# A four-layer graph network on one core: bias and fold products of the recurrent steps in the upper column half

## The reference, cut to what matters

```python
def step(feat, _):
    transformed = jnp.einsum('nd,khd->knh', feat, W) + b[:, None, :]
    msgs = transformed[etypes, src]
    a = jax.ops.segment_sum(msgs, dst, num_segments=num_nodes)
    feat = _gru_cell(a, feat, w_ih, w_hh, b_ih, b_hh)
    return (feat, None)
```

## Time and profile before

| | before |
|---|---|
| median of 3 runs | 13580.82 us |
| lowest and highest | 13574.45, 13581.73 us |
| the profiled execution | 13563.08 us |
| its span | 13561.3 us |
| TensorE, busy share of the span | 81% |
| VectorE, ScalarE, GpSimd | 41%, 26%, 32% |
| DMA queue q1, share of 16 engines | 39.6% |

### The profile page before, as it was taken

One profiled execution on the slowest core, in us unless ns is written; L12 is line 12 of the kernel. 1 busy time (PEld: TensorE's weight loads), 2 busy tenths in 40 slices (PEclk: granted clock), 3 DMA queues, 4 the chain that ended last, 5 costly groups with the idle time before them and its releaser, 6 DMA issues.

```text
span 13561.3 us, 260962 instructions
## 1 busy us (share of the span) xinstructions
PE 10980.6 (81%) x61679; PEld 6352.3 (47%) x61680; DVE 5577.2 (41%) x21369; ACT 3538.1 (26%) x9563; POOL 4391.2 (32%) x3429
## 2 busy tenths in 40 slices
PE   2888888799877777777777777775899999999999
PEld 2444444333335555555555555554644444444443
DVE  6888888766624333433343344343311111111111
ACT  0666666533302222222222222222100000000000
POOL 2000000000007888888888888885000000000000
PEclk7666676699889999999999999998699999999999
DMA  2444444422273333333333333336399899899898
GB/s 99 140 138 137 137 137 137 148 90 104 77 282 38 42 42 42 42 42 42 42 42 42 42 42 42 42 42 37 132 352 347 336 352 348 335 351 348 336 350 306
DMA packets 1120503, 2096.75 MB, mean 155 GB/s; under 512 B 373089, under 2 KB 982914, under 8 KB 1012531
## 3 DMA queue, kind: packets, MB, share of 16 engines
q1 hardware_dynamic: 823768, 1913.47, 39.6%
q0 software_dynamic: 295904, 174.34, 12.2%
HBM read 1630.21 MB, written 457.17 MB: 154 GB/s over the span
## 4 chain that ended last, share of the span: by engine, by line
PE 51%; issue 16%; POOL 13%; DMA 11%; DVE 4%; ACT 2%; SPq 1%; POOLq 0%; DVEq 0%; ACTq 0%
PE ps L1518 16%; PE ps L1147 11%; DMA reverse<-SD,sidx 11%; PE ps L1523 9%; POOL G L505 7%; POOL reverse L830 5%; PE ps L1203 2%; PE ps L1193 2%; DVE hots L1851 1%; PE ps L1211 1%; PE ps L1321 1%; ACT SD L939 1%; ACT stagebuf L860 1%; PE ps L1460 1%; PE ps L1326 1%
## 5 line engine op out<-in xcount | busy, mean ns | idle before, releaser
L830 POOL DMA_INDIRECT reverse<-SD,sidx x1660 | 2650.2, 1597 | 547.6 <-issue 493.2
L1518 PE MATMUL ps<-chunk,feat 128*128 128x512 f16 (+1 forms) x10192 | 2279.1, 375 | 14.4 <-DVE feat L2214 13.5
L505 POOL DMA_INDIRECT G<-h_table,idx x1660 | 1648.6, 993 | 1853.4 <-issue 1847.0
L1147 PE MATMUL ps<-hots 128*128 128x392 f16 x4859 | 1888.7, 446 | 433.8 <-issue 215.0
L1381 PE MATMUL ps<-MS,OH 128*128 128x128 f32 x3320 | 776.7, 317 | 1200.5 <-ACT SD L939 1194.3
L2051 DVE TENSOR_TENSOR acc<-acc,ps 128x132 f32 x1660 | 485.3, 292 | 2992.1 <-PE ps L1384 2975.1
L860 ACT ACTIVATE stagebuf<-ps 128x392 f32 x3248 | 1472.4, 506 | 883.9 <-PE ps L1150 805.2
L1518 PEld LDWEIGHTS ps<-chunk,feat 128*128 128x128 bf16 x10192 | 943.6, 98 | 1300.6 <-issue 307.3
L939 ACT ACTIVATE SD<-ps 128x129 f32<-128x129 f32 x1660 | 463.2, 279 | 3719.2 <-DMA reverse<-SD,sidx 3712.6
L1381 PEld LDWEIGHTS ps<-MS,OH 128*128 128x128 f32 x3320 | 546.5, 199 | 1749.8 <-issue 1726.1
L1370 PE MATMUL ps<-early,OT 128*128 128x256 f32 x3320 | 1086.2, 411 | 251.3 <-issue 221.9
(11 more groups left out here) (427 smaller groups left out, 14834.1 us busy)
## 6 DMA issues: line engine op xcount, KB each, us to landing
chunk<-adj SPq DMA_DIRECT2D x720, 1792.0 KB, 8.9
adj<-stagebuf SPq DMA_DIRECT2D x406, 784.0 KB, 5.7
chunkA<-adj SPq DMA_DIRECT2D x48, 1792.0 KB, 6.6
chunk<-adj SPq DMA_DIRECT2D x60, 1232.0 KB, 6.2
G<-in_edge SPq DMA_DIRECT2D x1660, 32.0 KB, 2.0
G<-h_table,idx POOLq DMA_INDIRECT x1660, 2.5
reverse<-SD,sidx POOLq DMA_INDIRECT x1660
reverse<-acc SPq DMA_DIRECT2D x4, 3225.0 KB, 20.0
```

Source lines behind the costliest of these rows:

```text
L505: nc.gpsimd.indirect_dma_start(G[:, j, 0:width], None, table, bass.IndirectOffsetOnAxis(idx[:, j:j + 1], 0))\
L830: nc.gpsimd.indirect_dma_start(reverse[j % R], bass.IndirectOffsetOnAxis(sidx[:, j:j + 1], 0), SD[:, j % R, :], None, compute_op=ALU.add). ...
L1147: nc.tensor.matmul(ps[:, bass.ds(window % 8 * 512, 2 * COMBS)], hots[:, j // HG % HRING, 0:P, j % HG], hots[:, j // HG % HRING, P:P + 2 * ...
L1518: nc.tensor.matmul(bank[k % 2][:, 0:cols], feat[0][:, hi, 0:2, :].rearrange("p a d -> p (a d)"), columns(chunk4, i % DRING, m, cols), star ...
```

## The change

- `biases`: the product goes to partitions 64 to 127 of the bank and starts a sum there (`start=True`). It takes 128 rows instead of 4; `counts` has 128 partitions, cleared once by VectorE ahead of the recurrent layer, and the SP load still fills 4 of them. `kb` is zero below its four rows.
- `fold`: the three products of the even nodes stay in the lower half, the three of the odd ones go to the upper half, and the loops are turned round, so that the two halves take turns.
- ScalarE's `aggregate` copies the upper half to a new tile `upper_agg`; VectorE's new `aggregate` adds the lower half to it, into the state tile. It stands ahead of `cell` in VectorE's program.
- the semaphore `raised` counts five copies a group instead of four.

```diff
-        counts = here("counts", [KT, 2, 512])
+        counts = here("counts", [P, 2, 512])
...
 def aggregate(n):   # ScalarE
...
-    nc.scalar.activation(AH[0:D, at_:at_ + cols], bank[2 + n % 2][0:D, 0:cols], ACT.Copy).then_inc(agg_out, 1)
+    if n:
+        act.wait_ge(agg_out, gb + n)
+    nc.scalar.activation(upper_agg[:, 0:cols], bank[2 + n % 2][D:P, 0:cols], ACT.Copy).then_inc(raised, 1)
...
 def biases(n):      # TensorE
...
-    return nc.tensor.matmul(bank[2 + n % 2][0:D, 0:cols], w("kb", KT), counts[:, n % 2, 0:cols],
-                            start=False, stop=False, skip_group_check=True)
+    return nc.tensor.matmul(bank[2 + n % 2][D:P, 0:cols], w("kb"), counts[:, n % 2, 0:cols],
+                            start=True, stop=False, skip_group_check=True)
 def fold(n):
...
-    for d in range(2):
-        for m in range(PARTS):
-            last = nc.tensor.matmul(bank[2 + n % 2][0:D, d:cols:2], overp4[0:OV, d, m, :], fold4[0:OV, n % 2, 0:cols // 2],
-                                    start=False, stop=d == 1 and m == PARTS - 1, skip_group_check=True)
+    for m in range(PARTS):
+        for d in range(2):
+            last = nc.tensor.matmul(bank[2 + n % 2][d * D:(d + 1) * D, d:cols:2], overp4[0:OV, d, m, :],
+                                    fold4[0:OV, n % 2, 0:cols // 2], start=False, stop=m == PARTS - 1, skip_group_check=True)
...
+            link(nc.vector.memset(counts[:, :, :], 0.0))     # VectorE, once
...
+                def aggregate(n):      # VectorE
+                    at_, cols = ORDER[n] * 512, 512 if n else P
+                    v.wait_ge(raised, rb + (n + 1) * (KT + 1))
+                    nc.vector.tensor_tensor(AH[0:D, at_:at_ + cols], bank[2 + n % 2][0:D, 0:cols], upper_agg[:, 0:cols], ALU.add)\
+                        .then_inc(agg_out, 1)
...
                 for n in range(2, NGRP):
                     hot4(n)
+                    aggregate(n - 1)
                     cell(n - 1)
```

More of the change, by code:

```diff
@@ L278, in build @@
         upper4 = here("upper4", [D, 2, 512])
+        upper_agg = here("upper_agg", [D, 512])
         kw2 = here("kw2", [P, KT // 2, D])
@@ L725, in _ @@
                         cols = 512 if n else P
-                        sp.dma_start(counts[:, n % 2, 0:cols], count_rows[:, ORDER[n] * 512:ORDER[n] * 512 + cols])\
+                        sp.dma_start(counts[0:KT, n % 2, 0:cols], count_rows[:, ORDER[n] * 512:ORDER[n] * 512 + cols])\
                             .then_inc(count_in[n % 2], 16)
@@ L998, in aggregate @@
                 def aggregate(n):
-                    at_, cols = ORDER[n] * 512, 512 if n else P
+                    cols = 512 if n else P
                     act.wait_ge(agg_done, gb + NGRP + n + 1)
-                    nc.scalar.activation(AH[0:D, at_:at_ + cols], bank[2 + n % 2][0:D, 0:cols], ACT.Copy).then_inc(agg_out, 1)
+                    if n:
+                        act.wait_ge(agg_out, gb + n)
+                    nc.scalar.activation(upper_agg[:, 0:cols], bank[2 + n % 2][D:P, 0:cols], ACT.Copy).then_inc(raised, 1)
                 def sigmoid(n):
@@ L2142, in _ @@
                 gb, sb4 = layer * NGRP, layer * (NGRP * KT)
+                rb = layer * (NGRP * (KT + 1))
                 def total(n, k):
@@ L2146, in total @@
                     half = slice(D, P) if k % 2 else slice(0, D)
-                    v.wait_ge(raised, sb4 + n * KT + k + 1)
+                    v.wait_ge(raised, rb + n * (KT + 1) + k + 1)
                     if n and k % 2 == 0:
@@ L2202, in _ @@
                     .then_inc(over_split, 1)
+                aggregate(0)
                 total(1, 0)
@@ L2211, in _ @@
                         total(n, k)
+                aggregate(NGRP - 1)
                 cell(NGRP - 1)
```

## The result

| | before | after |
|---|---|---|
| median | 13578.83 us (6 runs) | 13492.17 us (6 runs) |
| lowest and highest | 13572.25, 13581.73 | 13489.61, 13501.70 |
| profiled execution, its span | 13563.08, 13561.3 | 13491.83, 13490.1 |
| ratio to before | | 0.9937, 95% interval [0.9927, 0.9948] |

The change saves 87 us by the medians, with a 95% interval of 71 to 99 us from the ratio. Direction and place were right; the gain is 1.4 times the size forecast.

The account below looks back on a forecast made before the run. TensorE was taken to bound the recurrent layer; 56.8 + 1.9 + 2.2 - 0.95 = 59.9 us saved, which as a 0.44% share of the median gave 13521 us, with an 8-in-10 range of 13502 to 13557.

Parts of the forecast that it names:

- `biases`' first, in the other half, also at 0.43; its second at 0.86: Stretch from post to next chunk: biases starts with post's second instruction; 2.07 us instead of 3.36, 56.8 us over 44.
- the clearing: VectorE clears counts once ahead of the recurrent layer while TensorE waits; a cost of 0.95 us.
- more than forecast: Remaining case: a gain above the forecast, for instance after a shorter TensorE pause at step ends; chance 0.04.
- The change of row count: Passing between 128 or 112 rows and 4 rows around biases costs two drains; 128-row biases saves 0.21 us a stretch.
- Folds in pairs: In each stretch, lower and upper fold products run side by side, pairs 0.21 us apart, next chunk 0.35 after the last.
- Bare weight loads: In the no-overlap rival (0.12): uncovered weight loads add 1.07 us to the 2.07 us stretch, leaving 0.22 saved.
- all three rivals of less gain: One overlap kind fails (0.20), 13542 or 13553 us; overlap does nothing (0.12), 13574; slower through drains (0.04), 13605.
- that rival's second form: First rival (0.20, both forms): folds' alternate columns don't overlap; chunk at 2.72 us, 28 us saved, 13553 us.
- Group 0: First group of each step, taken apart: post and biases save 0.31 us, fold shrinks to 0.16; 0.47 a step, 1.9 together.
- Step ends: Fold's last starts 1.29 us sooner, uncovered VectorE add lengthens the hand-over to gates by 0.73; 0.56 saved, four times.
- Mid-step `aggregate` at no cost: VectorE's added aggregate in mid-step is covered by the chunk before gates; price nothing, 32 us if uncovered.
- `turn4`'s wait unchanged: TensorE's uncovered mid-step wait before turn4, 0.66 us in each of 44, moves with gates: neither better nor worse.

Follow-up runs that it names:

- e3: Kernel before, with biases taking 128 rows of counts (124 zero), still in the lower half, counts cleared once; ratio to the kernel before 0.9988.
- e4: Changed kernel with biases taking 4 rows again, in the upper half; median 13547.14 us, ratio to the kernel before 0.9979.
- e1: Changed kernel with the six fold products back in the lower half in their old order; median 13524.05 us, ratio to the kernel before 0.9962.
- e9: Changed kernel with each fold product written to neighbouring columns instead of every second one; median 13469.26 us, ratio to the kernel before 0.9927.
- e2: Changed kernel with the fold loops in their old order, three lower products then three upper; median 13491.24 us, ratio to the kernel before 0.9938.
- e5: Changed kernel with groups 1 to 12 ordered post, three lower folds, biases, three upper folds; median 13510.55 us, ratio to the kernel before 0.9953.
- e11: Changed kernel with four folds in the lower half, then two in the upper; median 13509.11 us, ratio to the kernel before 0.9948.

## Why the prediction was wrong, step by step

- "`biases`' first, in the other half, also at 0.43; its second at 0.86" is the step that failed. It took the order of issue as the order of starts: `post`'s second instruction ahead of `biases`' first. The runs show the halves starting on their own, so `biases` lies wholly beside `post` and `fold`'s pairs begin at 0.86, one 0.43 earlier: the stretch is 1.61 us and not 2.07. That term alone is 44 x 0.43 = 19 us, and 0.43 at each of four step ends, 1.7. With it the sum is 59.9 + 20.6 = 80.5 us, or 81.5 without the clearing, against 82.2 on the stage (3791.5 - 3709.3). I had no case on this side but "more than forecast" at 0.04, which made the range end too high.
- The change of row count: forecast 0.21 a stretch, though the prediction's own rows give 1.95 - 1.72 = 0.23; measured 0.25 (e3). What the Trainium skill states in "TensorEngine Tiling (Array Packing)", Key Properties, that a change of tiling mode drains the engine, agrees with e3 and with e4, where the 4-row product ran beside nothing. That these 124 rows of zeros would decide whether `biases` overlaps at all was not among the terms.
- Folds in pairs: the steps 0.21 apart and the 0.35 to the next chunk came as forecast; e1 to the changed kernel is 0.64 us. The first step from pair to pair is 0.17 and not 0.21, which is the 0.04 that is left of the 0.46 between 2.07 and 1.61. Bare weight loads would have put 1.07 us on the 2.07, by the prediction's own sum, and the whole stretch is 1.61. So what the Trainium skill states in "TensorE: Matmul & The Clock Gate", What overlaps and what doesn't, that weight loads overlap running matmuls only where the row group differs, is not what these traces show.
- Both overlaps in full: right, and with it all three rivals of less gain are out. The clue of the first, that the fold's half rate might have a reason that the halves share, is refuted: the reason is the output in every second column (e9), and the halves do not share it (e1 against the changed kernel). In that rival's second form the 2.72 does not follow from my own steps: with the first fold beside `biases` they give 2.50, so the two forms would have looked alike.
- Group 0: forecast 0.47 a step, measured 0.36 + 0.16 = 0.52.
- Step ends: forecast 0.56 each; measured 4.163 - 3.206 = 0.96, near to 0.56 plus the 0.43 above; `biases` starts 0.09 us behind `post` there (10673.14 after 10673.05). The 0.73 for the add came as worked out (1.37 - 0.64).
- Mid-step `aggregate` at no cost: right, no wait for L2161 but at the ends. The clearing: 0.91 us, forecast 0.92 and 0.03 for the link.
- `turn4`'s wait unchanged: nearly. In each step it is 0.36 us longer for one group, group 4, where VectorE starts on the sigmoid's result 0.36 us late. That is 1.4 us in all; its cause was not tried.
- One of the step ends before the change ran `gates` at the lower of the two clocks (granted 0.64 over 11633 to 11637, where it was 1.00 at the end of step 1), and took 1.6 us more. That counts in the 82.2 for the change by chance. With these two the terms add to 83.4: 77.3 + 2.1 + 3.8 + 1.6 - 1.4. Of the 1.2 us too much, 1.1 lie at the starts of steps 3 and 4, where after its pause TensorE stayed longer at the lower clock in the kernel after; such starts differ between the kernels run here, whatever the change. In step 3 the first products had a granted clock of 0.50 and took 4.22 us, where they had 0.55 and took 3.82 before.

## What to carry to other kernels

Lay out 64-column products as two queues, one for each half of the array, and take the longer one's time, not the order in which they stand; only keep partners close, since in these runs a pass five places on did not start early. Give a product of few rows full rows, even of zeros, before giving it another half: with 4 rows nothing ran beside it (e4). Then read what else TensorE waits for in the same stretch, since moving one call by one chunk brought 33 us here and the rearranged products 82.

## What the runs showed of the hardware that I had not expected

- Of two fp32 products in different column halves the second's first pass starts 3 ns after the first's, ahead of the first's second pass, and the pair takes 0.86 us, the time of one.
- TensorE starts a product of one half ahead of up to three that come before it in the program for the other half (two in e2, three in e5 and e11). The signal of the last one in the program still came after the product that it had overtaken (e11).
- A product of 4 rows between products of 128 or 112 costs 0.25 us a stretch, and runs beside nothing even in a half of its own (e3, e4).
- A product that writes every second PSUM column takes 0.22 us for 256 columns, and 0.11 with neighbouring ones (e9).
